# GRU preparation and opening rearranged, four value buffers, and masked keys of the last two groups written in place

## The reference, cut

```python
# x [128, 32, 256], cond [128, 256]
scale, shift = split(cond @ W_emb + b_emb)
xn = rms_norm(x, g_norm) * (1 + scale) + shift
q, k, v = heads(xn @ W_qkv)                  # 16 heads of 16
q, k = rms_norm(q, g_q), rms_norm(k, g_k)
o = softmax(q @ k.T * 16 ** -0.5) @ v
x = x + o + o @ W_out
# GRU over t, state h from cond
gi, gh = x[:, t] @ W_ih + b_ih, h @ W_hh + b_hh
r, z = sigmoid(gi_r + gh_r), sigmoid(gi_z + gh_z)
n = tanh(gi_n + r * gh_n)
h = (1 - z) * n + z * h
out[:, t] = x[:, t] + h
```

## Time and profile before

| | us |
|---|---|
| median of the runs (3) | 352.94 (352.61 to 353.09) |
| the profiled execution's own time | 350.47 |
| its span, first to last instruction | 348.4 |
| TensorE busy | 329.9 (95%) |
| VectorE busy | 252.7 (73%) |
| ScalarE busy | 237.6 (68%) |
| POOL busy | 220.5 (63%) |

### The profile page before, as it was taken

The page is one execution under the profiler, slowest core; times in us unless marked ns, Lnnn a source line. Parts: engine busy times, 40 slices in busy tenths (PEclk is TensorE's granted clock), DMA queues, the critical chain, the costliest instruction groups (busy, mean ns, idle before and its releaser), DMA issues.

```text
span 348.4 us, 12255 instructions
## 1 busy us (share of the span) xinstructions
PE 329.9 (95%) x4175; PEld 295.9 (85%) x4175; DVE 252.7 (73%) x666; ACT 237.6 (68%) x719; POOL 220.5 (63%) x402
## 2 busy tenths in 40 slices
PE   8798999999999999998978899999999999999994
PEld 7576687888888888887757899999999999999994
DVE  3667798899999999999875566555565666655555
ACT  4775777788888888886664366666666666666662
POOL 5587677787877787788653245555555555555552
PEclk9999999999999999999998899999999999999999
DMA  6963545333233333336340121122111111111111
GB/s 199 314 214 87 160 138 159 104 111 118 78 100 118 114 102 109 114 89 188 112 131 18 59 78 47 60 60 63 56 50 55 51 60 60 60 60 60 60 58 35
DMA packets 31911, 34.06 MB, mean 98 GB/s; under 512 B 5254, under 2 KB 26508, under 8 KB 31884
## 3 DMA queue, kind: packets, MB, share of 16 engines
q1 hardware_dynamic: 26108, 26.30, 25.1%
q10 hardware_dynamic: 5776, 7.41, 6.7%
HBM read 12.46 MB, written 8.39 MB: 60 GB/s over the span
## 4 chain that ended last, share of the span: by engine, by line
PE 74%; SPq 6%; DMA 5%; POOL 5%; issue 3%; ACT 3%; DVE 3%; ACTq 0%; POOLq 0%; DVEq 0%
PE bank L1184 38%; PE bank L1143 18%; PE bank L1300 4%; PE bank L1281 4%; PE bank L1269 3%; DMA v_diag<-v_rows 3%; SPq L396 3%; PE bank L1401 3%; SPq L388 3%; DMA operands<-operands 2%; PE bank L1261 2%; PE bank L1252 1%; POOL operands L459 1%; PE bank L1149 1%; POOL xn L470 1%
## 5 line engine op out<-in xcount | busy, mean ns | idle before, releaser
L1184 PE MATMUL bank<-wih_lo,wo_parts 128*128 128x256 f32 x192 | 56.6, 296 | 0.0
L1184 PE MATMUL bank<-wih_hi,wo_parts 128*128 128x256 f32 x192 | 54.0, 283 | 0.0
L1184 PE MATMUL bank<-wih_hi,pair_lo 128*128 128x256 f32 x192 | 53.3, 282 | 0.0
L1184 PE MATMUL bank<-wqkv_hi,hT_hi 128*128 128x256 f32 x192 | 53.3, 297 | 0.0
L580 POOL TENSOR_TENSOR operands<-operands,h 128x128 f32<-128x128 f32 x64 | 29.6, 463 | 35.8 <-ACT operands L849 35.5
L1184 PE MATMUL bank<-wqkv_lo,hT_hi 128*128 128x256 f32 x192 | 50.2, 281 | 0.0
L1143 PE MATMUL bank<-wqkv_hi,xn_hi 128*128 128x256 f32 (+1 forms) x126 | 47.4, 376 | 1.4 <-ACT v_rows L694 1.0
L1086 DVE TENSOR_TENSOR operands<-bank,operands 128x128 f32<-128x128 f32 x64 | 18.6, 291 | 40.0 <-ACT operands L846 40.0
L1184 PE MATMUL bank<-wqkv_hi,hT_lo 128*128 128x256 f32 x192 | 43.3, 282 | 1.6 <-DVE hT_lo L945 1.6
L1143 PE MATMUL bank<-wqkv_hi,xn_lo 128*128 128x256 f32 (+1 forms) x126 | 42.5, 338 | 0.0
L1143 PE MATMUL bank<-wqkv_lo,xn_hi 128*128 128x256 f32 (+1 forms) x126 | 42.5, 337 | 0.0
(11 more groups left out here) (128 smaller groups left out, 975.7 us busy)
## 6 DMA issues: line engine op xcount, KB each, us to landing
v_diag<-v_rows SPq DMA_DIRECT2D x128, 34.0 KB, 1.9
operands<-operands SPq DMA_DIRECT2D x64, 64.0 KB, 2.0
operands<-operands SPq DMA_DIRECT2D x32, 128.0 KB, 2.1
out_dram<-x ACTq DMA_DIRECT2D x16, 256.0 KB, 2.5
w_emb_sb<-out_dram SPq DMA_DIRECT2D x32, 128.0 KB, 2.1
out_dram<-w_emb_sb SPq DMA_DIRECT2D x31, 128.0 KB, 1.7
x_in<-in_x_dram SPq DMA_DIRECT2D x7, 512.0 KB, 7.3
stage_w<-in_L_cond_W_ih_dram ACTq DMA_DIRECT2D x2, 384.0 KB, 3.5
```

Of the source, the lines that this page charges most:

```text
L1184: return pe.matmul(dst, moved, gate_columns(weights, k, block), start=False, stop=True, skip_group_check=True)
```

## The change

What it does, part by part:

- Opening. ScalarE makes the shift (`shifts`), VectorE no longer; the cast and the low part of the second half of W_qk are POOL's, ahead of its pipeline; the second pair's Newton steps are VectorE's. The condition's products are signalled in two halves. TensorE has 14, 5 and 12 warming products instead of 11, 3 and 8. The first value projection starts before the low part of W_v is there.
- v_rows has four buffers, v_diag_ready four semaphores, and the wait of L692 is gone.
- Biases have their own space, with the sum in the order of b, not of the banks, and are loaded in four broadcasts in turns 6 to 9; POOL sums them in one instruction in turn 11. `set_gates` reads them in bank order.
- W_ih is cast in turns 10 and 11 by ScalarE, wih_lo is made by POOL in four halves in turns 32 to 35. W_hh's low halves are POOL's turns 37, 37, 38 and 39. The first state is split in turns 10 and 11.
- Groups 30 and 31: no masked copy and no key DMA. Each strip of 32 partitions is written in place: strip 0 by POOL (turns 36, 37), strips 1 and 2 by VectorE (turns 35, 36, ahead of the row maxima), strip 3 by ScalarE in two instructions (turns 35, 36).
- TensorE does group 31's scores first in turn 38 and its output projection first in turn 41; VectorE does group 31's attention output ahead of a residual. The state's products move to turns 39, 40 and 41; six unread products go there, four are added ahead of the second banks' clearing.

Cut diff:

```diff
-        biases = x_in[:, 0:6, :].rearrange("p g d -> p (g d)")[:, 0:6 * D].rearrange("p (i f) -> p i f", i=2)
-        bias_n = biases[:, :, 2 * D:3 * D]
-        bias_rz = x_in[:, 6:8, :].rearrange("p g d -> p (g d)")[:, 0:2 * D].rearrange("p (c f) -> p c f", c=KC)
+        biases = sb("biases", [P, 2, 2 * D])
+        bias_n = biases[:, 1, :].rearrange("p (i f) -> p i f", i=2)
+        bias_sum = biases[:, 0, :].rearrange("p (g c a) -> p c g a", g=2, c=KC)
+        bias_other = stage_wo[:, :, :].rearrange("p c f -> p (c f)")
...
-        v_rows = sb("v_rows", [P, 2, HEADS, VW])
+        v_rows = sb("v_rows", [P, 4, HEADS, VW])
...
+        def strip_keys(slot, first, count, r=slice(0, 2)):
+
+            rows = slice(PB * first, PB * first + PB * count)
+            return (rows, k_diag[rows, slot, first in (1, 2), r, :, :].rearrange("p r j k -> p r (j k)"),
+                    qkT[rows, slot, D:2 * D])
...
-                if g is not None:
+                if g is not None and not direct(g):
                     place_keys(g, (u - SP_KEYS) % 2)
                 v = group(base, u, SP_V)
                 if v is not None:
-                    place_values(v, (u - SP_V) % 2, (u - SP_V) % 4)
+                    place_values(v, (u - SP_V) % 4)
...
+            def direct_strips(k, slot):
+                rows, place, keys = strip_keys(slot, 0, 1)
+                pool.wait_ge(qkT_ready, k + 1)
+                pool.tensor_tensor(place, keys.unsqueeze(1).broadcast_to([PB, 2, D]),
+                                   gqk_parity[rows, :].unsqueeze(2).broadcast_to([PB, 2, D]),
+                                   ALU.mult).then_inc(direct_keys[slot], 1)
...
+            def summed_biases():
+                for done, count in bias_loaded:
+                    pool.wait_ge(done, count)
+                pool.tensor_tensor(biases[:, 0, :], biases[:, 0, :], bias_other, ALU.add).then_inc(bias_ready, 1)
+
+            def gate_weights(c, half):
+                cols = slice(half * 3 * P, half * 3 * P + 3 * P)
+                pool.wait_ge(wih_hi_ready, c + 1)
+                pool.tensor_tensor(wih_lo[:, c, cols], stage_w[:, c, cols], wih_hi[:, c, cols].bitcast(F32),
+                                   ALU.subtract).then_inc(wih_ready, 1)
...
                 if k is not None:
-                    mask_keys(k, (u - POOL_KEYS) % 2)
+                    if direct(k):
+                        direct_strips(k, (u - POOL_KEYS) % 2)
+                    else:
+                        mask_keys(k, (u - POOL_KEYS) % 2)
+                for i in range(2 * KC):
+                    if turn_is(base, u, NG + i):
+                        gate_weights(i // 2, i % 2)
+                    if turn_is(base, u, NG + PE_QKT + (0, 0, 1, 2)[i]):
+                        state_weights(i // 2, i % 2)
+                if turn_is(base, u, FIRST_LOOPED - 1):
+                    summed_biases()
...
-                for i in range(2 * KC):
-                    if turn_is(base, u, NG + POOL_XLO + 3 + i):
-                        state_weights(i // 2, i % 2)
-                if turn_is(base, u, NG + POOL_XLO):
-                    summed_biases()
...
-            def second_norms():
-                second = [norm_first[:, i, FIRST_PAIR:FIRST_NORMED] for i in range(7)]
-                pool.wait_ge(rs0_ready, LAG_QK)
-                pool.tensor_tensor(second[4], second[3], second[3], ALU.mult).then_inc(newton_step, LAG_QK)
-                pool.wait_ge(newton_step, LAG_QK)
-                pool.tensor_tensor(second[5], second[4], second[0], ALU.mult).then_inc(newton_step, LAG_QK)
-                pool.wait_ge(newton_step, 2 * LAG_QK)
-                pool.tensor_tensor(second[4], threes[:, 0:FIRST_PAIR], second[5], ALU.subtract)\
-                    .then_inc(newton_step, LAG_QK)
-                pool.wait_ge(newton_step, 3 * LAG_QK)
-                pool.tensor_tensor(second[6], second[4], second[3], ALU.mult).then_inc(rs_ready, LAG_QK)
+            pool.wait_ge(qk_loaded[1], 16)
+            pool.tensor_copy(wqkv_hi[:, 1, 0:2 * D], stage_w[:, 1, 0:2 * D]).then_inc(wqk_hi_ready[1], 1)
+            pool.wait_ge(wqk_hi_ready[1], 1)
+            pool.wait_ge(first_norm, 6)
+            pool.tensor_tensor(wqkv_lo[:, 1, 0:2 * D], stage_w[:, 1, 0:2 * D], wqkv_hi[:, 1, 0:2 * D].bitcast(F32),
+                               ALU.subtract).then_inc(wqk_ready, 1)
...
+            act.wait_ge(qk_loaded[0], 16)
+            act.copy(wqkv_hi[:, 0, 0:2 * D], stage_w[:, 0, 0:2 * D]).then_inc(wqk_hi_ready[0], 1)
...
+            def shifts():
+                act.wait_ge(vec_cols_ready, 1)
+                act.wait_ge(emb_ps, 2)
+                for c in range(KC):
+                    last = act.activation(mod_shift[:, c, :, :].rearrange("p g b -> p (g b)"),
+                                          p_s[:, BANK + c * B:BANK + c * B + B], ACT.Identity,
+                                          bias=bemb[:, KC + c:KC + c + 1])
+                last.then_inc(mod_ready, 1)
+
+            def second_squares():
                 act.wait_ge(x_loaded[0], 16)
                 first_squares(FIRST_PAIR, FIRST_NORMED)
+
+            def second_norms():
...
-            def gate_weights():
-                act.wait_ge(ih_loaded, 16 * KC)
-                act.copy(wih_hi[:, :, :], stage_w[:, :, :]).then_inc(wih_hi_ready, 1)
+                act.dma_start(staged[:, i % KC, :], source[(i % KC) * P:(i % KC) * P + P, :]).then_inc(loaded[i % KC], 16)
+
+            def gate_weights(c):
+                act.wait_ge(ih_loaded[c], 16)
+                act.copy(wih_hi[:, c, :], stage_w[:, c, :]).then_inc(wih_hi_ready, 1)
...
-            def load_biases():
-                act.wait_ge(x2_ready, 8)
-                for i, vector in enumerate((b_hh, b_ih)):
-                    act.dma_start(biases[:, i, :], vector.unsqueeze(0).broadcast_to([P, 3 * D])).then_inc(bias_loaded, 16)
+            def load_bias(i):
+
+                if i == 0:
+                    act.wait_ge(wo_ready, 1)
+                vector, cols, space = ((b_ih, slice(0, 2 * D), bias_other), (b_hh, slice(0, 2 * D), biases[:, 0, :]),
+                                       (b_hh, slice(2 * D, 3 * D), bias_n[:, 0, :]),
+                                       (b_ih, slice(2 * D, 3 * D), bias_n[:, 1, :]))[i]
+                act.dma_start(space, vector[cols].unsqueeze(0).broadcast_to(list(space.shape)))                   .then_inc(bias_loaded[i][0], 16)
 
...
             def set_gates(e):
-                act.copy(rz_banks[e], bias_rz[:, :, :]).then_inc(rz_set, 1)
+                act.copy(rz_banks[e].rearrange("p c (g a) -> p c g a", g=2), bias_sum).then_inc(rz_set, 1)
                 act.copy(n_banks[e].rearrange("p (i f) -> p i f", i=2), bias_n).then_inc(n_set, 1)
...
-                if later(v, 2):
-                    act.wait_ge(v_diag_ready[slot], spread(v - 2, slot, GB))
...
+            def direct_strips(k, slot):
+                act.wait_ge(qkT_ready, k + 1)
+                for r in range(2):
+                    rows, place, keys = strip_keys(slot, 3, 1, slice(r, r + 1))
+                    act.activation(place[:, 0, :], keys, ACT.Copy, scale=gqk_parity[rows, r:r + 1])\
+                       .then_inc(direct_keys[slot], 1)
...
+                elif first:
+                    act.wait_ge(second_norm, 4)
                 else:
-                    act.wait_ge(rs_ready, LAG_QK if first else n + 1)
+                    act.wait_ge(rs_ready, n - LAG_QK + 1)
...
-                if turn_is(base, u, NG + ACT_QKT):
-                    gate_weights()
+                for c in range(KC):
+                    if turn_is(base, u, FIRST_LOOPED - KC + c):
+                        gate_weights(c)
                 g = group(base, u, ACT_QKT)
                 if g is not None:
                     queries_keys(g, (u - ACT_QKT) % 2)
+                k = group(base, u, PE_QKT)
+                if k is not None and direct(k):
+                    direct_strips(k, (u - PE_QKT) % 2)
...
+                    shifts()
                     scaled_input(1, 1)
-                    projection_weights(1)
-                    second_norms()
+                    second_squares()
...
-                if turn_is(base, u, NG):
-                    load_biases()
+                for i in range(4):
+                    if turn_is(base, u, FIRST_LOOPED - 6 + i):
+                        load_bias(i)
...
-                if turn_is(base, u, NG - 2 + ACT_OT):
+                if turn_is(base, u, FIRST_LOOPED - 2):
                     first_state()
+                if turn_is(base, u, NG - 3 + ACT_OT):
                     act.wait_ge(bias_ready, 1)
                     act.wait_ge(gates_clear[0], 1)
                     set_gates(0)
...
+            def second_norms():
+                second = [norm_first[:, i, FIRST_PAIR:FIRST_NORMED] for i in range(7)]
+                dve.wait_ge(rs0_ready, LAG_QK)
```

(51 more changed lines are left out.)

118 lines of the change are left out of this document (63 added, 55 removed).

## The result

| | before | after |
|---|---|---|
| median of the runs (8 each), us | 352.77 (351.55 to 353.57) | 350.25 (348.57 to 351.51, one at 361.61) |
| the profiled execution's own time, us | 350.47 | 349.43 |
| its span, us | 348.4 | 347.5 |

The account below looks back on a forecast made before the run. TensorE was taken to bound the middle of attention and the recurrence, so time could move only in the opening and drain: -1.3 - 2.3 + 0.3 - 0.8 - 0.6 - 3.6 = -8.3 us, giving 344.6 us, range 341.6 to 349.0.

Parts of the forecast that it names:

- Part 1: Opening to 26.4 us: first norms earlier through work moved between VectorE, ScalarE and POOL, -1.3 us, bounds -0.5 and -1.9.
- Part 2: 26.4 to 73 us: four v_rows buffers remove ScalarE's waits, -2.3 us; added broadcasts, casts, state and bias sum, +0.3.
- The opening doesn't gain: Rival, chance 0.13: key DMAs sharing engines with broadcasts and W_ih loads end late, casts fill turns 10 and 11; 346.6 us.
- Part 3 (a): Drain: bias broadcasts gone, group 27's key wait -1.1 us, wih_lo on POOL +0.3; net -0.8.
- +0.3 as charged: Drain, turns 32 to 35: POOL's halves of wih_lo make oT_lo late for TensorE, +0.3 us, bounds 0 and +1.5.
- (b): Drain: direct strips for groups 30 and 31 replace key DMAs, net -0.6 us, bounds +1.0 and -2.6.
- The rival: Drain, chance 0.20: VectorE's four strips each wait out a POOL instruction, 0.6 us on average, 2.4 in all.
- (c): Behind the last probsT: first state, state products and last output projection moved, -3.6 us, bounds -2 and -4.5.
- the first piece: End of drain: first state on VectorE no longer delays the last output projection, 2.1 us.
- A longer recurrence: Rival, chance 0.05: gate biases read in four pieces in 31 steps; each 0.1 us more would cost 3.1 us.
- Strips meet POOL: Rival, chance 0.20: VectorE's strips in the drain wait for POOL, oT_lo is late; gain only 5.5 us, 347.4.
- the opening's 3.3: Up to group 9: -1.3 us from first norms, -2.3 from four v_rows buffers, +0.3 for work added there.

Follow-up runs that it names:

- the two edits that moved this load: Changed kernel, W_hh's halves in turns 38, 39, 40, 40, plus: first unrolled part 16 turns, not 12 (346.87 us, 0.9887); or weight loads one turn later (347.08 us, 0.9884).
- (b) repaired: Changed kernel with W_hh's halves behind oT_lo in turns 38, 39, 40, 40 and direct strips for group 31 alone: 345.89 us, ratio 0.9842, drain 119.7.
- The best ratio, 0.984: Changed kernel, W_hh's halves in turns 38, 39, 40, 40, plus weight loads one turn later, more unread products, strips for group 31 alone: 345.46 us.
- the second kernel with later broadcasts: Changed kernel with bias broadcasts in turns 10 and 11, their sum in turn 36, and W_hh's halves behind oT_lo: 351.55 us, ratio 0.9999.

## Why the prediction was wrong, point by point

**Part 1 (-1.3): right.** Group 0's scores come at 25.25 against 26.41, 1.16 earlier. What the norms decide repeats: SP issues the keys of group 0 at 21.84 to 22.84 us in all sixteen kernels with the new first part, and at 23.12 and 23.46 in the two with the old one. What follows does not: the scores of group 0 lie between 25.15 and 26.83 in the fifteen others, after waits of 0.2 to 1.6 us for those keys, against 27.27 in the second old one. So about 1 us of this part is real, and luck decides how much of it a given execution shows.

**Part 2 (-2.3, +0.3): wrong, by 3 us with what follows.** I had two terms. Groups 0 to 3 were to go from 14.56 to 14.0 us; they took 16.21. Groups 3 to 9 were to go from 32.03 to 30.3; they took 31.48.

The step that failed in the first term is "What is late next is SP's queue up to group 3, whose 4.43 us a turn is unchanged, and TensorE after it". SP's queue is next, but its pace is not the landing, and for the time from first issue to scores I had allowed nothing over what the row of before had. For group 2 that was 4.06 us, with TensorE arriving at 35.97 and no wait. In after TensorE is ready at 33.91, 2.06 us earlier. With 4.06 us it would have waited 0.9: so much of the latency had been hidden behind a late TensorE. The time was 5.01 instead, so the keys also landed 0.95 later. Then the clock fell, which the sum of part 2 didn't have, and took another 1.7 us. Three key issues also take 1.86 us in one turn and 2.5 to 2.8 in another (31.91 before, 30.76 after), so the pace of the queue is not a constant either.

Why the keys landed later is in part argued. In ten profiles the first load of W_ih is issued less than 3 us behind the first key of group 2, and its scores start 4.45 to 6.74 us behind that key; an eleventh has 4.09. In the seven where the load is issued more than 3.1 us behind, or turns later, they start 4.00 to 4.43 us behind it, once 4.81. That is the mechanism which I had put under "The opening doesn't gain": without its own wait ScalarE loads earlier, into the keys. But the two edits that moved this load bring no gain in total (ratios of 0.9887 and 0.9884 against 0.9857), because later keys wait instead. How much SP's queue, ScalarE's transfers and the keys' own latency each take stays open, since equal openings differ by up to 2.9 us at group 15.

The step that failed in the second term is "From group 3 on every turn is full". No profile of the study has less than 31.48 us from group 3 to group 9, the kernel before with four buffers alone 31.53. In after two of these turns are long without any wait for a key, 5.35 and 5.90 us against 5.06. In the longer one VectorE's split of the first state, which the change put there, takes 1.12 us beside POOL's mask, and TensorE waits 0.54 for probsT behind it; that turn was 5.67 before. What the four buffers are worth inside the changed kernel was not measured: no kernel has the change without them.

**Part 3 (a) (-0.8): right.** Group 27 waits for no key DMA; group 25 to group 27 is 10.38 us instead of 11.22. Two turns with wih_lo cost 0.14 each (5.18 and 5.20 against 5.05), +0.3 as charged.

**(b) (-0.6, at worst +1.0): wrong, and the largest miss in the drain.** With (a) it made the time from group 25's scores to group 31's attention products 2.3 us longer (34.32 to 36.59) where 1.4 less were forecast; without strips it is 33.66. Two steps failed. "POOL then casts low halves of W_hh in the same turn, 2 us before oT_lo, and can hold VectorE: +0.7" priced only the side of VectorE. The halves stand ahead of oT_lo in POOL's order and wait for ScalarE's cast, which itself stands behind the strips; TensorE paid 3.29 us. And an order of TensorE, output projection ahead of group 31's scores, made these scores wait for it, 3 us beyond the logits of group 30, the last thing they needed. Two edits show it, each of which leaves the other part of the pair in place: without strips the ratio is 0.985, with the halves one turn later 0.9857, both clear of the change's 0.9925. VectorE's pair of strips took 2.08 us for group 31 and 1.40 for group 30. The rival had about the right price for a pair that meets POOL, but only one of the two does; "POOL's queue has free time in turns 36 and 38" was true and no help. The Trainium skill, "SBUF — State Buffer", section "SBUF: two separate sides", says that such a pair of instructions excludes each other for the whole instruction. By that rule, the trace agrees in direction only: two strips (1.40 alone) and two halves (1.96 alone) need 3.36 us one after the other, and together they took 2.94.

**(c) (-3.6): nearly right.** From group 31's attention products to the pair's cast it was 9.93 us, it is 6.95, a gain of 3.0; without strips it is 6.95 too. The state products no longer stand in the way, but the last projection still waits 0.37 us for oT_lo. Of the first piece, the first state on VectorE (2.1), the experiment shows 1.3 by the middle, with intervals that overlap.

**The rivals.** A longer recurrence: false, 147.10 against 147.30. "Strips meet POOL" (347.4) and "the opening doesn't gain" (346.6) came both, and each was dearer than priced. I gave each a chance of its own and none to both together, which is 349.4 by my own prices (2.8 and 2.0 us over the forecast). The opening's was made dearer by the clock that fell behind the stall, which my sum had nowhere. The drain's was not: the granted clock is 0.50 at 184 to 186 us in both profiles, with 1.7 us missing around it in both, and the second fall of before, at 192 to 198 us, is gone as (c) had it.

The drain's part of the forecast was not out of reach: with (b) repaired it is 4.9 us shorter than before in the profile, where 5.0 were forecast. The total was never reached. The best ratio, 0.984, is 5.6 us of the 352.77 that before took beside the change, and 8.3 were forecast; the opening's 3.3 stayed away in all kernels (group 15 at 102.02 at best, where 100.0 was needed).

## What to carry to other kernels

Price a step that is put ahead of another on an in-order engine by who waits for the second one, and follow its own wait back (here POOL's halves waited for ScalarE, and TensorE paid), not by its duration. Where one removed wait had covered a transfer, take the transfer's whole latency as the next limit, and not the queue's pace, and ask what the engine that no longer waits will issue earlier, and into what (here ScalarE's W_ih load, into the keys). Where two rivals can both come true, give their sum a chance.

## What the hardware showed

A stall of TensorE can cost more than itself, and its length alone does not say whether it will. After the 1.86 us wait for group 2 the granted clock was half until about 39.9 us; after one of 3.60 us (the same place, in the kernel with strips for group 31 alone) it was this:

```profile
34.00:38.00 4.00, 0.54 (x32) 0.43 (x32) 0.97 (x2) 0.95 (x4) 1.75 (x6) 1.00 0.67 193
38.00:42.00 4.00, 4.00 (x54) 3.37 (x44) 3.18 (x7) 1.88 (x5) 1.13 (x2) 0.57 0.33 95
```

In the opening waits of 1.80 (no strips), 1.83 and 2.17 (the second kernel with later broadcasts), 2.04, 2.63 and 3.60 us for keys were followed by such a fall as well. Waits of 1.67 and 2.15 (halves one turn later) and of 1.89 (broadcasts on SP's queue) were not, and the clock stayed at 1.00. Nor did it fall behind a wait of 2.93 us for the keys of group 31 in the kernel before with four buffers, where it fell behind 1.97 in the kernel before itself. Each of the seven falls of the opening took the same, 1.7 us of clock, whether the wait was 1.80 or 3.60 us.

A strip on 32 partitions took VectorE 0.70 us and POOL 1.03, about what 128 partitions of as many elements take them (0.65 to 0.69 and 1.04): a strip saves no time by being narrow.
